# Attention and the Hadamard feed-forward network of an adaLN layer in one block: the weight transform moved beside the last heads and onto the rows, weights streamed

## What is computed

```python
def _layernorm(x, axis=-1, eps=1e-05):
    m = jnp.mean(x, axis=axis, keepdims=True)
    v = jnp.var(x, axis=axis, keepdims=True)
    return (x - m) / jnp.sqrt(v + eps)
...
        q = (hidden_states @ q_w.T + q_b).reshape(b, s, H, HEAD_DIM)
        k = hidden_states @ k_w.T + k_b
        v = hidden_states @ v_w.T + v_b
        scores = jnp.einsum('bqhd,bkd->bhqk', q, k) / HEAD_DIM ** 0.5
        causal = jnp.triu(jnp.ones((s, s), dtype=bool), k=1)
        scores = jnp.where(causal[None, None], -jnp.inf, scores)
        attn = jax.nn.softmax(scores.astype(jnp.float32), axis=-1).astype(q.dtype)
        out = jnp.einsum('bhqk,bkd->bqhd', attn, v).reshape(b, s, H * HEAD_DIM)
        return out @ o_w.T + o_b
...
        x = fwht(x * SU_ug) / SCALE
        x_up = x @ W_up.T * (Wscale_ug[:INTER] * SCALE)
        x_gate = x @ W_gate.T * (Wscale_ug[INTER:] * SCALE)
        x = jax.nn.silu(x_gate) * x_up
        x = fwht(x * SU_dp) / SCALE
        x = x @ W_down.T * (Wscale_dp * SCALE)
...
    h = _layernorm(x, axis=-1) * (1 + ca) + sa
    x = x + ga * _L0_attn_ref(h, L0_attn_q_w, L0_attn_q_b, L0_attn_k_w, L0_attn_k_b, L0_attn_v_w, L0_attn_v_b, L0_attn_o_w, L0_attn_o_b)
    h = _layernorm(x, axis=-1) * (1 + cb) + sb
    x = x + gb * _L0_ffn_ref(h, L0_ffn_SU_ug, L0_ffn_SU_dp, L0_ffn_Wscale_ug, L0_ffn_Wscale_dp, L0_ffn_W_up, L0_ffn_W_gate, L0_ffn_W_down)
    return x
```

## Time and profile before

| | us |
|---|---|
| median of 3 runs | 2211.45 |
| lowest and highest | 2208.47, 2212.17 |
| the profiled execution's own time | 2208.33 |
| its span in the trace | 2206.7 |

### The profile page before, as it was taken

One profiled execution on the slowest core, in us unless ns is written; L12 is line 12 of the kernel. 1 busy time (PEld: TensorE's weight loads), 2 busy tenths in 40 slices (PEclk: granted clock), 3 DMA queues, 4 the chain that ended last, 5 costly groups with the idle time before them and its releaser, 6 DMA issues.

```text
span 2206.7 us, 28816 instructions
## 1 busy us (share of the span) xinstructions
PE 2036.4 (92%) x9552; PEld 1521.7 (69%) x9552; DVE 1321.2 (60%) x2742; ACT 963.4 (44%) x1540; POOL 220.4 (10%) x546
## 2 busy tenths in 40 slices
PE   6999999999999999963689999999999999999998
PEld 5666667666666666651268788787887878878786
DVE  5676675767577666726954654646446464554644
ACT  2256552655365534611444344443434434444322
POOL 0011121111111111204400000000000000000000
PEclk9799999999999999986789999999999999999999
DMA  7142344324432343238000100101001010010000
GB/s 234 46 130 69 88 107 117 78 60 121 116 77 62 88 126 78 65 103 294 0 1 0 39 0 0 38 0 38 0 0 38 0 38 0 0 38 0 20 0 19
DMA packets 71775, 128.48 MB, mean 58 GB/s; under 512 B 22774, under 2 KB 28022, under 8 KB 71552
## 3 DMA queue, kind: packets, MB, share of 16 engines
q1 hardware_dynamic: 69504, 118.93, 19.2%
q0 software_dynamic: 2176, 8.39, 1.1%
HBM read 65.12 MB, written 19.15 MB: 38 GB/s over the span
## 4 chain that ended last, share of the span: by engine, by line
PE 44%; DVE 3%; issue 1%; DMA 1%; ACT 1%; DVEq 0%; SPq 0%; ACTq 0%
PE banks L1285 30%; PE banks L1294 14%; DVE w_ring L1217 1%; DMA out<-out_sb 1%; DVE out_tmp L1264 0%; DVE out_sb L1266 0%; DVE h_t_split L1211 0%; ACT w_ring L1153 0%; PE banks L1277 0%; DVE h_t_split L1212 0%; DVE ln_stats L1193 0%; DVE y L1243 0%; ACT silu_gate L1171 0%; DVE y_split L1249 0%; DVE d_ring L1222 0%
## 5 line engine op out<-in xcount | busy, mean ns | idle before, releaser
L1285 PE MATMUL banks<-h_t_split,w_ring 128*128 128x512 f32 x3072 | 722.7, 391 | 15.3 <-DVE w_ring L1217 8.9
L1285 PEld LDWEIGHTS banks<-h_t_split,w_ring 128*128 128x128 f32 x3072 | 576.9, 188 | 144.0 <-DVE w_ring L1217 14.8
L530 ACT ACTIVATE probs<-banks 128x512 f32<-128x512 f32 x576 | 314.7, 597 | 162.7 <-PE banks L875 162.4
L1294 PE MATMUL banks<-d_ring,y_split 128*128 128x512 f32 x1536 | 370.5, 390 | 0.1
L1294 PEld LDWEIGHTS banks<-d_ring,y_split 128*128 128x128 f32 x1536 | 287.2, 188 | 59.4 <-DVE y_split L1250 0.5
L1243 DVE SCALAR_TENSOR_TENSOR y<-banks,scale_upgate,silu_gate 128x512 f32<-128x512 f32 x128 | 96.1, 751 | 360.1 <-ACT silu_gate L1171 360.1
L896 PE MATMUL banks<-probs,v_ones 128*64 128x128 f32 (+3 forms) x1920 | 297.0, 439 | 0.2 <-POOL probs L573 0.2
L832 PE MATMUL banks<-k_stack,q_stacks 96*128 96x512 f32 (+3 forms) x768 | 249.3, 369 | 15.9 <-DVE q_split L615 11.1
L875 PE MATMUL banks<-q_stacks,k_stack 98*128 98x512 f32 (+3 forms) x768 | 255.0, 375 | 0.0
L896 PEld LDWEIGHTS banks<-probs,v_ones 128*64 128x64 f32 x1920 | 146.3, 138 | 152.3 <-issue 124.3
L1171 ACT ACTIVATE silu_gate<-banks,scale_upgate 128x512 f32<-128x512 f32 x128 | 88.2, 689 | 357.4 <-PE banks L1285 356.9
(11 more groups left out here) (126 smaller groups left out, 1666.6 us busy)
## 6 DMA issues: line engine op xcount, KB each, us to landing
q_stacks<-q_split SPq DMA_DIRECT2D x192, 128.0 KB, 2.4
o_group<-o_raw SPq DMA_DIRECT2D x128, 128.0 KB, 2.4
x<-in_x SPq DMA_DIRECT2D x32, 256.0 KB, 3.2
o_group<-inverse_sums_dram SPq DMA_DIRECT2D x64, 128.0 KB, 2.7
x_and_residual<-in_x SPq DMA_DIRECT2D x32, 256.0 KB, 3.4
x_dram<-x_and_residual SPq DMA_DIRECT2D x32, 256.0 KB, 2.5
x_in<-x_dram POOLq DMA_DIRECT2D x8, 1024.0 KB, 6.1
out<-out_sb SPq DMA_DIRECT2D x32, 256.0 KB, 2.0
```

The costliest lines, as they stand in the source:

```text
L530: nc.scalar.activation(pr[:, u, :], score_bank[:, at % SLOTS_SCORE, :], ACT.Exp, scale=SCALE).then_inc(exped, 1)
L1285: last = nc.tensor.matmul(bank[side][:, s, :], wr[s][a][:, k, side, :], ht[:, m, k, :], start=(k == 0 and a + m == 0), stop=(k == KT - 1 a ...
L1294: last = nc.tensor.matmul(acc[t // 2][:, t % 2, :], ys[s][:, a, t * P:(t + 1) * P], dr[s][m][:], start=(first and a + m == 0), stop=(last_ ...
```

## The change

- **One block.** The three phases become one, `phase`; buffers of the network lie in memory that the attention no longer uses (the names `under_...` are place holders in that layout). Loops are gone: all 128 steps of the network stand in line, with the step's number g.
- **The up and gate weights are not transformed.** Instead each block's modulated rows are: two butterfly stages on DVE (`cross`, four instructions of 128 x 1024), a split (`round_crossed` on ACT, `crossed_rest` on DVE) and a Hadamard product on PE in float32r (`had_tile`, two matmuls for each of four tiles, L1269), rounded and split again. The signs are folded into the modulation.
- **The down weights are transformed beside the heads** as 32 new side items, `FOLDS`: 16 `across` in heads 45 to 50 (one float32 product with a 128 x 128 matrix, L1252), 16 `along` in heads 54 to 59 (two float32r matmuls, L1257). Each is rounded by ACT (`fold_halves`), its rest taken by DVE (`fold_rest`), stored by SP (`store_fold`, 512 KB) to DRAM. `across` items are loaded by `load_raw` (256 KB), `along` items by `load_again` (512 KB), two ahead, each load issued behind the store two items earlier.
- **Weights are streamed.** Each step loads 512 KB of raw up and gate weights (ring of 3, rounded and split as before) and 512 KB of ready split down weights (ring of 4), all by SP. The rounding and subtraction of the down weights (L1177, L1222) go.
- **The first block is prepared beside the last heads**: layer norm in heads 59 and 60, `turn` (four transposes a tile) in head 61, `cross` in 62, `had` in 63. The other blocks are prepared in the middle of the block before (`beside(g)`: `turn` in steps 6 and 7, `had` in 11 and 12), ahead of `down(g - 1)`; behind it PE waits until the banks that it lent are read (`beside_read(g)`).
- **The last batch's projection** goes into steps 3, 4, 5, 8, 9, 10, 13 and 14 of block 0.
- **Outputs**: DVE reads each tile of the result as it is done, from the step after.
- The start has five more small loads (the Hadamard matrix, signs, scales) and a few small DVE instructions in `later`.

The diff, cut to what the steps above name:

```diff
+FOLDS = [("across", left, u) for left in (19, 18, 17, 16) for u in (3, 5, 7)] + [("across", left, u) for left in (15, 14) for u in (4, 7)]
+FOLDS += [("along", left, u) for left in (10, 9, 8) for u in (3, 5, 7)] + [("along", 7, 7)]
+FOLDS += [("along", left, u) for left in (6, 5) for u in (3, 5, 7)]
+BLOCK_IN, STAT_LEFT, NORM_LEFT, TURN_LEFT, CROSS_LEFT, HAD_LEFT = 6, 5, 4, 3, 2, 1
+TURN_UNITS, HAD_UNITS = (2, 4, 6, 8), (1, 2, 3, 4)
...
+TURN_STEPS, HAD_STEPS = {6: (0, 1), 7: (2, 3)}, {11: (0, 1), 12: (2, 3)}
+TAIL_TILES = {3: 0, 4: 1, 5: 2, 8: 3, 9: 4, 10: 5, 13: 6, 14: 7}
+NT = HALF // P
...
+            def load_raw(i):
+                if i >= 2:
+                    side_filled(sp, ("across", i - 2))
+                sp.dma_start(raw[:, i % 2, :], io["w_down"].rearrange("(q j) n -> j q n", j=FT)[i]).then_inc(raw_in[i % 2], 16)
+            def load_again(i):
+                if i == 0:
+                    for n in range(2):
+                        sp.wait_ge(fold_out[n], 16 * FT // 2)
+                if i >= 2:
+                    side_filled(sp, ("along", i - 2))
+                sp.dma_start(again[:, i % 2].bitcast(F32), across_rows[i * P:(i + 1) * P]).then_inc(again_in[i % 2], 16)
+            def store_fold(key):
+                kind, i = key
+                side_taken(sp, key)
+                to = across_rows.rearrange("(q j) a n -> j q a n", j=FT)[i] if kind == "across" else down_rows[i * P:(i + 1) * P]
+                sp.dma_start(to, fold[:, i % 2].bitcast(F32)).then_inc(fold_out[i % 2], 16)
+                if i + 2 < FT:
+                    (load_raw if kind == "across" else load_again)(i + 2)
...
+            def load_upgate(g):
+                if g >= UG_RING:
+                    sp.wait_ge(ug_ready, g - UG_RING + 1)
+                sp.dma_start(ugr[g % UG_RING][:], io["w_ug"][g % FT]).then_inc(ug_in[g % UG_RING], 16)
+            def load_down(g):
+                if g == 0:
+                    sp.wait_ge(scored, ALL * NU)
+                    for n in range(2):
+                        sp.wait_ge(fold_out[n], 16 * FT)
+                if g >= D_RING:
+                    sp.wait_ge(d_done, g - D_RING + 1)
+                sp.dma_start(dr[g % D_RING][:].bitcast(F32), down_rows[g % FT * P:(g % FT + 1) * P]).then_inc(d_in[g % D_RING], 16)
...
+            def network(g):
+                blk, f = divmod(g, FT)
+                if g + UG_RING < STEPS:
+                    load_upgate(g + UG_RING)
+                if 2 <= g + 2 < STEPS and g:
+                    load_down(g + 2)
+                if f == X_STEP:
+                    if blk:
+                        store_block(blk - 1)
+                    if blk + 1 < BLOCKS:
+                        load_block(blk + 1)
+                if blk == 0 and f in TAIL_TILES:
+                    store_tile(B - 1, TAIL_TILES[f])
+                if g == FT - 1:
+                    sp.wait_ge(x1_ready, B * TT)
+                    sp.dma_start(gbw[:], gains_dram[1:2].to_broadcast([P, B, D])).then_inc(gbw_in, 16)
...
+            def fold_rest(key):
+                kind, i = key
+                dve.wait_ge(fold_hi, (FT if kind == "along" else 0) + i + 1)
+                r, hi, lo = slot(key)[0], fold[:, i % 2, 0, :], fold[:, i % 2, 1, :]
+                scale = su[:, KT + i:KT + i + 1] if kind == "along" else 1.0
+                nc.vector.scalar_tensor_tensor(out=lo, in0=side[:, r, :], scalar=scale, in1=hi.bitcast(F32),
+                                               op0=ALU.mult, op1=ALU.subtract).then_inc(side_free[r], 1)
...
+            def fold_tile(key):
+                kind, i = key
+                if kind == "across":
+                    pe.wait_ge(across_in, 16)
+                    pe.wait_ge(raw_in[i % 2], 16 * (i // 2 + 1))
+                    r = side_slot(key)
+                    last = nc.tensor.matmul(side[:, r, :], across[:], raw[:, i % 2, :], start=True, stop=True)
+                else:
+                    pe.wait_ge(again_in[i % 2], 16 * (i // 2 + 1))
+                    r = side_slot(key)
+                    for a in range(2):
+                        last = nc.tensor.matmul(side[:, r, :], had[:], again[:, i % 2, a, :], start=a == 0, stop=a == 1)
+                last.then_inc(side_full[r], 1)
...
+            def up_gate(g):
+                blk, f, s = g // FT, g % FT, g % 2
+                pe.wait_ge(ug_ready, g + 1)
+                if g == 0:
+                    for k in range(KT):
+                        side_taken(pe, ("had", k))
+                    pe.wait_ge(exped, ALL * NU)
+                elif f == 0:
+                    pe.wait_ge(ht2_lo, blk * KT)
+                if g == 1:
+                    side_drained(pe, 0)
+                if g >= 2:
+                    pe.wait_ge(y_mul, g - 1)
+                for n, bank in enumerate((up_bank, gate_bank)):
+                    last = product(bank[:, s, :], lambda a, k: wr[s][:, a, k, n, :], lambda m, k: fht[blk % 2][:, m, k, :], KT)
+                last.then_inc(ug_done, 1)
+            def beside(g):
+                blk, f = divmod(g, FT)
+                nb, ahead = blk + 1, blk + 1 < BLOCKS
+                if ahead and f in TURN_STEPS or ahead and f in HAD_STEPS or blk == 0 and f in TAIL_TILES:
+                    pe.wait_ge(y_mul, g)
+                if ahead and f in TURN_STEPS:
+                    for k in TURN_STEPS[f]:
+                        turn(nb, k, free_bank(g, k)).then_inc(turned, 1)
+                if ahead and f in HAD_STEPS:
+                    for k in HAD_STEPS[f]:
+                        had_tile(nb, k, free_bank(g, k)).then_inc(had_done, 1)
+                if blk == 0 and f in TAIL_TILES:
+                    project(B - 1, TAIL_TILES[f], free_bank(g, 0)).then_inc(projected, 1)
+            def beside_read(g):
+                blk, f = divmod(g, FT)
+                if blk + 1 < BLOCKS and f in TURN_STEPS:
+                    pe.wait_ge(h2_ready, blk * KT + TURN_STEPS[f][-1] + 1)
+                if blk + 1 < BLOCKS and f in HAD_STEPS:
+                    pe.wait_ge(ht2_lo, blk * KT + HAD_STEPS[f][-1] + 1)
+                if blk == 0 and f in TAIL_TILES:
+                    pe.wait_ge(tail_read, TAIL_TILES[f] + 1)
+            def down(g):
+                blk, f, s = g // FT, g % FT, g % 2
+                pe.wait_ge(y_ready, g + 1)
+                pe.wait_ge(d_in[g % D_RING], 16 * (g // D_RING + 1))
+                if g == 0:
+                    for r in (1, 2):
+                        side_drained(pe, r)
+                    for c in range(2):
+                        pe.wait_ge(o_copied[c], ALL)
+                elif f == 0:
+                    pe.wait_ge(acc_read, blk * NT)
+                for t in range(NT):
+                    for a, m in ((0, 0), (0, 1), (1, 0)):
+                        last = nc.tensor.matmul(acc[:, t, :], ys[s][:, a, t * P:(t + 1) * P], dr[g % D_RING][:, m, :],
+                                                start=(f == 0 and a + m == 0), stop=(f == FT - 1 and a == 1))
+                    if f == FT - 1 and t < NT - 1:
+                        last.then_inc(acc_done, 1)
+                last.then_inc(d_done, 1)
...
             weigh(ALL - 1, THIRD - 1)
+            for g in range(STEPS):
+                up_gate(g)
+                if g:
+                    beside(g)
+                    down(g - 1)
+                    beside_read(g)
+            down(STEPS - 1)
```

816 lines of the change are left out of this document (394 added, 422 removed).

## The result

| | median us | range of its runs | ratio to before |
|---|---|---|---|
| before | 2211.81 | 2208.47 to 2212.29 | |
| after | 2156.00 | 2151.30 to 2158.64 | 0.9748 (95% interval 0.9729 to 0.9768) |

The change makes the kernel 2.5% faster. The forecast was 2115 us, 4.4% faster: the sign is right, the size is 41 us off, and 2156 lies near the upper end of the range. The profiled execution took 2156.94 us, its span 2155.2.

The account below looks back on a forecast made before the run. PE was taken to bound heads and network, with a 168.6 us gap between. 950.4 + 0.7 + 50 + 9, + 1092.5 + 1.5, + 6.3 gave 2110.4 us of span; with 1.6 and 3.1 more, 2115 us, range 2080 to 2160.

Parts of the forecast that it names:

- rival B: Heads and steps cost more: items hold ring banks (75 instead of 50), step waits add 13; 2153 us, chance 0.20.
- Step 1: Between last weigh and first up_gate: the 168.6 us gap goes, its contents coming back elsewhere.
- rival D: Network start still waits for the last group's result: up to 11 us come back, 2126 us; chance 0.05.
- Steps 2 and 5: Network: batch 3's projection +24.2 us; other seven blocks' had +12.6, boundary waits gone; 1092.5 instead of 1079.4 us.
- Step 3: Down transform beside the heads: PE work 21.3 us plus load waits and restarts, +50 us, bounds 18 and 75.
- Step 4: Block 0's preparation beside the last heads: norm 3, turn 3.2, had 1.8, a wait 1; +9 us.
- Step 6: Start of the network: DVE runs the last group's scaling between the steps, +1.5 us.
- Step 7: End of the kernel: 6.3 instead of 8.3 us, DVE reading the first three tiles while down still runs.
- Step 8: Prologue: +0.7 us for a few small DVE instructions ahead of the first maxima.
- Step 9: Network: down weights' rounding and subtraction, the loops and the 1 MB a step stream change nothing.
- The check on the tops: Expected distances between heads' tops: 12 to 14 us in heads 45 to 47, 54, 55, 58, 59; near 20 in 48, 56.
- three signs of being wrong: Steps longer than 8.3 us, head 48 without a wait, or first steps waiting for DVE by more than 3 us.

Follow-up runs that it names:

- e1: The kernel after with deeper load rings for the down items (fold_raw four buffers, fold_again three, instead of two each): 2123.4 us, ratio 0.9614.
- e4: The kernel after without any down-transform item, the network streaming as many bytes from another buffer (output not the reference's): 2066.9 us, ratio 0.9350.
- e9: The kernel after with only the table of places changed, two items in each of sixteen heads instead of three in ten: 2097.0 us, ratio 0.9492.
- e12: e9 with the load of block 0 (x_in, 1 MB) one head earlier, behind head 57 instead of 58: 2092.5 us, ratio 0.9472.
- e11: e9 plus e1's rings and early item stores ahead of the inverses, with the third up and gate weight also asked for earlier: 2097.1 us, ratio 0.9479.

## Why the prediction was right and where it was not

That 2156 falls into the range, whose upper end is 2160, is in part luck. The sum itself was 41 us off, and the upper end came from rival B's 2153, which counts 13 us of waits in the network's steps that never appeared. For the stretch from head 44 on, steps 3 and 4 had 59 us, and 100.5 came:

| us | forecast | measured |
|---|---|---|
| PE work at full clock (21.3 + 1.6 + 1.8) | 24.7 | 27.6 |
| lower clock while PE is busy | 3 | 20.2 |
| PE idle (in the forecast all that is left of the 59: waits, less the slack) | 31.3 | 52.7 |

- **Step 1, the gap: right.** It goes to the last microsecond; `up_gate` follows at full clock, and rival D did not come.
- **Steps 2 and 5, the network: right.** Sixteen steps of a later block take 134.2 us against 134.0, a step with a projection 11.1 against 11.2, a step 8.16, and no step behind the start has a wait of PE that the profile lists. The rows of a busy loop (8.16 us, 0.227 a matmul) could be carried over to the code without a loop as they were.
- **Step 3, the items: the term that failed.** 50 us were taken, 75 was the upper bound, and 85.5 were measured. Its PE work was near, 21.3 against 24.0. Its mechanism was right, and it stood in the right heads with the right releasers. Four sizes were wrong. The waits for loads were put at 28.4 us and are 40.9: in head 48 the inverses themselves came 2.9 us later behind the head's top, and 512 KB read back landed in 5.3 us instead of 4. A loss of clock was counted behind the two long waits alone, 3 us; it lay behind short ones as well, 2.7 us behind one of 3.2, and came to 13.4 us for the items. The hold of a bank was put into the bound only and not into the value; the waits for it are 6.3 us in after and 13.5 in e1. And 3 us of slack were taken off that nothing gave back: in the plain head of the earlier trace rows PE is idle 0.1 of the 9.78 us, and not 1. As a bound, 75 counted the hold but left the waits at their first size.
- **Rival B: right by its time (2153), wrong by its cause.** It had the heads 25 us and the steps 13 us dearer. The steps cost nothing, and of the heads' excess the hold of banks is the small part: 6.3 us of waits against 40.9 for loads. In its argument the page's stall is narrower than it reads there: the Trainium skill, "Runtime: NRT & Kernel Launch", section "Instruction fetch mechanics", ties it to a branch whose target lies outside the instructions already fetched, so a looped step without a gap doesn't speak against it.
- **Step 4, block 0's preparation: 9 against 15.0** (e4). Its PE work was right, 3.4 against 3.6; the rest is 4.6 us of idle time, where the sum had 5.6, and 6.8 of lower clock, for which it had nothing. Of the idle time, 3.5 us are waits of PE for POOL's masked `probs` in the last two heads (3.9 in after, 0.2 before). They have no maxima left to fill in with; that this makes the wait is argued, not shown. Of the lower clock, 1.5 us are in head 44, where it is 0.93 and no new wait stands. It falls at 711.99 us, ahead of the first load for the items (716.30), after 9 us in which PE was busy 8.18 us, and 8.17 in the same 9 us before, where the clock stayed at 1.00. Why is open; it falls in every kernel of this structure, without items too.
- **Step 6, the start: 1.5 against 4.1,** a wait of 2.57 us and 7.17 - 5.6 = 1.57 of lower clock, which e9 to e12 don't have behind waits of 0.68 to 2.52 us. The cause was another: VectorE's subtraction was late because ScalarE, ahead of it, waits 9.6 us for `upgate_raw`, and not through VectorE's own work. The step's pull on the time is small, as e11 showed.
- **Step 7, the end: 5.9 against 6.3.** Step 8, 0.7 for the prologue: the part ahead of head 44 is 697.7 us before and after, and 693.7 to 699.3 in the other kernels, so no run can tell it. Step 9: no wait for a streamed weight behind the start.
- **The check on the tops:** 18.4, 14.1 and 14.4 in heads 45 to 47, and 17 to 20 in the along heads, where I wrote 12 to 14; "near 20" in heads 48 and 56 forgot the q projection in that stretch (15.15 before); by my own sum it should have read 27, and it was 32. "The clock stays 1.00" was wrong up to the network: 0.92 from 700 us to its start. None of the three signs of being wrong appeared.
- **The landing times.** The waits of heads 45 to 47 did not vanish: they are 4.5 us, with 256 KB landing in 3.7. The Trainium skill, "DMA: Bandwidth & Descriptors", section "Anatomy of one DMA", gives the line from which step 3 has 2.6 for transfers that GpSimd issues; the loads here are issued by SyncE.

## What to carry to other kernels

Work put beside a full engine costs its own time on that engine as long as each piece's buffer, store and bank are back before its turn; ask of every piece which of the three comes back last and what stands ahead of it on the queue. If that answer is "the piece before last of the same head", spread the pieces out first: a table of places was worth more here (59 us) than deeper rings (33) or a better order on the queue (23), and made both needless. Price a wait with what it can do to the clock behind it, short ones too: here between nothing and 3 us each, and 20 us in sum.

## What the hardware showed

- The clock behind waits: 0.56 over the 6.2 us that follow a wait of 3.20 us, 0.79 over the 11.8 us that follow 10.95. That wait of 3 us cost 6. Others cost only themselves: behind 2.54 us in after (head 62) the clock was 1.00.
- A load of 512 KB that was written shortly before by the same queue lands in 5.3 us (5.8 in e1 and e9, 5.5 in e12), a load of the same size of the ready down weights in the network in 3.3, and one of raw up and gate weights there in 4.3. I had taken them all as one. Whether it is the fresh write, or the store that runs beside it at a DMA share of up to 0.90, the runs don't tell apart. The Trainium skill, "DMA: Bandwidth & Descriptors", section "Anatomy of one DMA", gives 2.0 us plus the bytes at 436 GB/s for transfers that GpSimd issues, which would be 3.2 us for 512 KB; these are issued by SyncE. The 3.3 agrees with it; the 4.3, the 5.3, and the 3.7 of `fold_raw` against its 2.6 for 256 KB, do not, and the measurement decides.
- A stream of 141 GB/s beside 1098 us of nearly unbroken matmuls costs them nothing that can be measured: a step is 8.16 us with it and without. Nor does straight code cost anything, some 9,000 PE instructions in a row in place of a loop.
